# Tanh layer of a graph network: expansion in fp32 on 32 rows of the array, products as the stationary operand of the contraction, gathers not held back

## What is computed

```python
xs = concatenate([x[src, :8], x[dst, :8]])                 # 16 scalars of an edge
xv = concatenate([x[src, 8:], x[dst, 8:]])                 # 16 vectors of 3
h = 2.0 ** 0.5 * relu(emb @ W1 / 10.0 ** 0.5)              # 16 hidden values of an edge
w = (h @ W2 / 16.0 ** 0.5).reshape(E, 7, 16, 8)            # weights of an edge
s_out = PW_S * (einsum('eu,euw->ew', xs, wa_s) + INV_SQRT3 * einsum('eui,ei,euw->ew', xv, y1, wb_s))
g_out = PW_S * (einsum('eu,euw->ew', xs, wa_g) + INV_SQRT3 * einsum('eui,ei,euw->ew', xv, y1, wb_g))
v_out = PW_V * (...)                                       # 8 vectors of 3, from wc, wd and we
edge_ftr = concatenate([TANH_GAIN * tanh(s_out), TANH_GAIN * tanh(g_out)[:, :, None] * v_out]) * norm
out = segment_sum(edge_ftr, dst)
```

## Time and profile before

| | |
|---|---|
| median of 3 runs | 14886.34 us (14883.05 to 14889.52) |
| the profiled execution: its time, its span | 14891.23 us, 14889.4 us |
| the Tanh layer's pass, first to last expansion | 4499.3 to 9755.5 us |
| instructions in the span | 427370 |
| busy: PE, PEld, DVE, ACT, POOL | 79%, 61%, 87%, 53%, 67% |
| granted TensorE clock, mean of the span | 0.888 |

### The profile page before, as it was taken

One profiled execution on the slowest core, in us unless ns is written; L12 is line 12 of the kernel. 1 busy time (PEld: TensorE's weight loads), 2 busy tenths in 40 slices (PEclk: granted clock), 3 DMA queues, 4 the chain that ended last, 5 costly groups with the idle time before them and its releaser, 6 DMA issues. The chain is left out here.

```text
span 14889.4 us, 427370 instructions
## 1 busy us (share of the span) xinstructions
PE 11746.5 (79%) x109342; PEld 9054.7 (61%) x109342; DVE 12928.2 (87%) x30182; ACT 7888.3 (53%) x23572; POOL 9996.3 (67%) x10549
## 2 busy tenths in 40 slices
PE   1555555555548999999999999979788888888888
PEld 1444444444446666666666666667666666666666
DVE  5777777777768999999999999977799999999997
ACT  0555555555536666666666666638344444444443
POOL 4777777777756666666666666638577777777775
PEclk8666666666669999999999999979899999999999
DMA  3555555555542222222222222238211111111111
GB/s 94 84 87 87 86 87 86 87 87 87 87 67 38 36 36 36 36 36 36 36 36 36 36 36 36 36 116 293 57 24 24 24 24 24 24 24 24 24 24 23
DMA packets 2705891, 840.21 MB, mean 56 GB/s; under 512 B 2232498, under 2 KB 2650073, under 8 KB 2704124
## 3 DMA queue, kind: packets, MB, share of 16 engines
q1 hardware_dynamic: 2212179, 616.76, 20.7%
q0 software_dynamic: 312320, 178.52, 9.2%
q10 hardware_dynamic: 181250, 43.25, 1.3%
HBM read 610.22 MB, written 226.58 MB: 56 GB/s over the span
## 5 line engine op out<-in xcount | busy, mean ns | idle before, releaser
L1352 POOL DMA_INDIRECT w_rows<-table,w_idx x9375 | 8929.7, 952 | 4086.9 <-issue 2387.3
L1583 PE MATMUL w_p_w<-w_w,w_ht 128*128 128x256 f32 x12500 | 3007.2, 388 | 125.1 <-DVE w_prodv L1527 124.5
L1335 PE MATMUL w_p_deg<-w_hot_lo,w_hot_row 128*128 128x196 bf16 x6250 | 1797.5, 336 | 1573.4 <-DVE w_hot_lo L1280 1535.0
L1583 PEld LDWEIGHTS w_p_w<-w_w,w_ht 128*128 128x128 f32 x12500 | 2273.1, 190 | 673.5 <-issue 299.4
L1147 ACT ACTIVATE w_dist<-row_iota,w_negrel 128x32 f32<-128x32 f32 x9375 | 2182.6, 315 | 300.1 <-issue 272.2
L1554 ACT ACTIVATE w_ht<-w_p_h 128x512 f32<-128x512 f32 x1875 | 851.2, 526 | 2489.6 <-PE w_p_h L1574 2489.6
L1793 DVE TENSOR_TENSOR w_prod<-w_p_xe,w_he 128x512 f32<-128x512 f32 x3125 | 2137.5, 684 | 4.3 <-PE w_p_xe L1936 4.3
L1309 ACT CAST w_counts<-w_p_count 128x784 uint8<-128x784 f32 x1875 | 1247.2, 706 | 1453.3 <-PE w_p_count L1336 1435.9
L1335 PEld LDWEIGHTS w_p_deg<-w_hot_lo,w_hot_row 128*128 128x128 bf16 x6250 | 829.9, 133 | 1698.1 <-issue 1607.8
L1336 PE MATMUL w_p_count<-w_hot_lo,w_hot_row 128*128 128x196 bf16 x6250 | 1808.6, 336 | 0.0
L1959 PE MATMUL w_p_sgt<-w_prod,w_wc 128*32 128x128 f32 x25000 | 1331.6, 284 | 85.9 <-ACT w_sgt L1872 65.7
(11 more groups left out here) (211 smaller groups left out, 20273.9 us busy)
## 6 DMA issues: line engine op xcount, KB each, us to landing
counts<-w_counts SPq DMA_DIRECT2D x1250, 122.5 KB
d_small<-counts SPq DMA_DIRECT2D x388, 392.0 KB
w_rows<-table,w_idx POOLq DMA_INDIRECT x9375
w_rel_row<-rel_row SPq DMA_DIRECT2D x625, 120.0 KB
w_edge<-e SPq DMA_DIRECT2D x625, 80.0 KB
w_idx<-src SPq DMA_DIRECT2D x1875, 2.5 KB
w_negrel<-negrel SPq DMA_DIRECT2D x1875, 2.5 KB
w_nodes<-split SPq DMA_DIRECT2D x1875, 2.0 KB
```

Source lines behind the costliest of these rows:

```text
L1335: nc.tensor.matmul(p_deg[:], hot_row[s2][:, b, :], hot_lo[s2][:, b, :], start=False, stop=False, skip_group_check=True)
L1352: pool.indirect_dma_start(out=rows[:, t, :], out_offset=None, in_=table[0:N, :], in_offset=bass.IndirectOffsetOnAxis(ap=idx[:, t:t + 1], a ...
L1583: last = nc.tensor.matmul(p_w[(g.base * len(BANKS) + bank) % WBANKS][:, (t - t0) * 256:(t - t0 + 1) * 256], ht[g.slot(UNROLL)][:, k, t * P ...
```

## The change

Four things change in `window_pass_1`; the other layers keep their code.

1. The values are no longer split. PE turns `x32` itself, in fp32: five matmuls with `x32` (128 x 32) stationary and the fp32 identity moving, tile t into partitions 32 (t mod 4) of `p_xt`. ACT copies the result as fp32, in two instructions. Gone are ACT's two casts and DVE's two subtractions of a step.
2. `expand` multiplies in fp32: `pick_c` (32 x 128, on the partitions of the tile's strip) stationary, 128 columns of `xt` on the same 32 partitions moving; four matmuls a tile as before.
3. `contract` takes `prod` (128 x 128 fp32) as stationary operand and `wc` (24 columns) moving; four matmuls add up in `p_out[:, t, :]`, where the edges are on partitions at once. `p_sgt`, `sgt`, `stack`, ACT's two copies of a step and the five turning matmuls are gone; ACT takes tanh from `p_out` and copies its last 8 columns to `along`, from which DVE's L1826 now reads.
4. The five gathers of a group are issued without `wait_count` on the tile products.

```diff
@@ POOL
-                    for t in range(T):
-                        wait_count(pool, prod_ready, g.times(T, t - 3 * T))
-                        pool.nop(nofuse=True)
-                        gather_tile(pool, a["table"][1], idx[s], rows[s], t, gathered[s])
+                    pool.nop(nofuse=True)
+                    gather_rows(pool, a["table"][1], idx[s], rows[s], gathered[s])
@@ DVE
-                if g := at(2):
-                    vec.tensor_sub(rest[s2][:], x32[s2][:], xs[s2][:, :, 0, :]).then_inc(rest_ready, 1)
...
-                    vec.tensor_mul(prodv..., spread(p_out[:, :, T_AT:SGT], [P, T, 8, 3], 3),
+                    vec.tensor_mul(prodv..., spread(along[s2][:], [P, T, 8, 3], 3),
...
-                    vec.tensor_sub(xs[s2][:, :, 2, :], rest[s2][:], xs[s2][:, :, 1, :]).then_inc(low_ready, 1)
@@ ACT
                 if g := at(4):
-                    activate(g, 4, T)
+                    act.wait_ge(tile_out, g.times(T, T))
+                    nc.scalar.activation(bent[s2][:], p_out[:, :, 0:G_ROWS], ACT.Tanh, scale=1.0 / 32 ** 0.5).then_inc(bent_ready, 1)
+                    nc.scalar.copy(along[s2][:], p_out[:, :, T_AT:OUT]).then_inc(along_ready, 1)
...
-                    nc.scalar.copy(xt[g.slot(2)][0:SPLIT * 32, :], p_xt[:, 0:GE]).then_inc(xt_ready, 1)
-                if g := at(3):
-                    free(act, out_ready, g, 2)
-                    activate(g, 0, 4)
+                    nc.scalar.copy(xt[s2][:, 0, :], p_xt[:, 0, :])
+                    nc.scalar.copy(xt[s2][0:32, 1, :], p_xt[0:32, 1, :]).then_inc(xt_ready, 1)
@@ PE, expand
+                rows = slice(t % 4 * 32, t % 4 * 32 + 32)
                 for i in range(4):
-                    last = nc.tensor.matmul(p_xe[b][:, i * P:(i + 1) * P], pick_b[:, i, :], xt[g.slot(2)][:, t * P:(t + 1) * P],
+                    last = nc.tensor.matmul(p_xe[b][:, i * P:(i + 1) * P], pick_c[rows, i, :], xt[g.slot(2)][rows, t // 4, :],
                                             start=True, stop=True)
@@ PE, contract
                 for i in range(4):
-                    last = nc.tensor.matmul(p_sgt[QUAD * i:QUAD * (i + 1), t % 4 * P:(t % 4 + 1) * P], wc[:, i, :], prod[b][:, i, :],
-                                            start=True, stop=True)
-                last.then_inc(sgt_tile, 1)
+                    last = nc.tensor.matmul(p_out[:, t, :], prod[b][:, i, :], wc[:, i, :], start=i == 0, stop=i == 3)
+                last.then_inc(tile_out, 1)
@@ PE, step
-                if g := at(4):
-                    done(pe, sgt_last, g)
-                    for t in range(T):
-                        last = nc.tensor.matmul(p_out[:, t, :], sgt[g.slot(2)][:, t * P:(t + 1) * P], stack[:],
-                                                start=True, stop=True)
...
-                    for e in range(T):
-                        last = nc.tensor.matmul(p_xt[:, e * P:(e + 1) * P], xs[g.slot(2)][:, e, :, :].rearrange("p s i -> p (s i)"),
-                                                ident_b[:], start=True, stop=True)
+                    for t in range(T):
+                        last = nc.tensor.matmul(p_xt[t % 4 * 32:t % 4 * 32 + 32, t // 4, :], x32[g.slot(2)][:, t, :], a["ident"][:], start=True, stop=True)
```

More of the change, by code:

```diff
@@ L1658, in window_pass_1 @@
         dots = [sb(f"dots{s}", [P, T, MUL1, 3]) for s in range(2)]
-        xs = [sb(f"xs{s}", [P, T, SPLIT, 32], BF16) for s in range(2)]
-        rest = [sb(f"rest{s}", [P, T, 32]) for s in range(2)]
-        xt = [sb(f"xt{s}", [P, GE], BF16) for s in range(2)]
+        xt = [sb(f"xt{s}", [P, 2, P]) for s in range(2)]
         he = [sb(f"he{s}", [P, GE]) for s in range(UNROLL)]
@@ L1666, in window_pass_1 @@
         redv = sb("redv", [P, T, 24])
-        sgt = [sb(f"sgt{s}", [P, GE]) for s in range(2)]
         bent = [sb(f"bent{s}", [P, T, G_ROWS]) for s in range(2)]
-        stack = sb("stack", [P, WIDE])
+        along = [sb(f"along{s}", [P, T, 8]) for s in range(2)]
         gate = [sb(f"gate{s}", [P, T, 16]) for s in range(2)]
@@ L1723, in _ @@
         def _(pool):
-            pool.memset(pick_f[:], 0.0).then_inc(picks, 1)
+            pool.memset(pick_c[:], 0.0).then_inc(picks, 1)
             for b in range(4):
[L1727 to L1730, removed]
+                for q in range(4):
+                    pool.wait_ge(picks, 4 * b + q + 1)
+                    view = pick_c[:, b, :].rearrange("p (u h) -> p u h", h=HID1)
+                    pool.affine_select(out=view, in_=view, compare_op=ALU.not_equal, fill=1.0, base=-(32 * q + 8 * b),
                                        pattern=[[-1, 8], [0, HID1]], channel_multiplier=1).then_inc(picks, 1)
@@ L1791, in tile_products @@
                 dve.wait_ge(xe_ready, g.times(T, t + 1))
-                wait_count(dve, sgt_tile, g.times(T, t - 1))
+                wait_count(dve, tile_out, g.times(T, t - 1))
                 vec.tensor_mul(prod[b][:], p_xe[b][:].rearrange("p (i e) -> p i e", e=P),
@@ L1867, in _ @@
         def _(act):
[L1868 to L1872, removed]
             def step(at):
                 if g := at(4):
-                    activate(g, 4, T)
-                if g := at(2):
                     s2 = g.slot(2)
-                    done(act, q_ready, g)
-                    free(act, xt_mm, g, 2)
-                    nc.scalar.copy(xs[s2][:, :, 0, :], x32[s2][:]).then_inc(high_ready, 1)
+                    act.wait_ge(tile_out, g.times(T, T))
+                    free(act, gate_ready, g, 2)
+                    free(act, vout_ready, g, 2)
+                    nc.scalar.activation(bent[s2][:], p_out[:, :, 0:G_ROWS], ACT.Tanh, scale=1.0 / 32 ** 0.5).then_inc(bent_ready, 1)
+                    nc.scalar.copy(along[s2][:], p_out[:, :, T_AT:OUT]).then_inc(along_ready, 1)
                 if g := at(1):
@@ L1974, in step @@
                     expand(g, 1)
-                if g := at(4):
-                    done(pe, sgt_last, g)
-                    pe.wait_ge(dst_copied, g.times(1, 3) if at(2) else G)
-                    free(pe, w.acc_added, g, 1)
-                    for t in range(T):
-                        last = nc.tensor.matmul(p_out[:, t, :], sgt[g.slot(2)][:, t * P:(t + 1) * P], stack[:],
-                                                start=True, stop=True)
-                    last.then_inc(out_ready, 1)
-                if g := at(3):
-                    contract(g, 0)
-                    expand(g, 2)
-                    vector_weights(g, 0, 1)
                 if g := at(1):
@@ L1999, in step @@
                 if g := at(3):
+                    contract(g, 0)
+                    expand(g, 2)
+                    vector_weights(g, 0, 1)
                     contract(g, 1)
```

75 lines of the change are left out of this document (23 added, 52 removed).

## The result

The changed kernel takes 25106.54 us (median of 4 runs, 25097.27 to 25109.12); the kernel before, on the same chip, 14885.82 us (4 runs). The ratio is 1.687, 95% interval 1.684 to 1.689. Slower was forecast, but 18,280 us with a range of 17,500 to 20,500; the time lies near the rival with the lower clock (27,300 us).

What follows compares the result with a forecast made beforehand. PE was taken to bound the changed layer: 4.45 + 4.45 + 1.13 + 0.36 + 0.2 + 1.06 + 2.2 = 13.85 us a step against 8.42, over 625 steps 3394 us more: 18,280 us, range 17,500 to 20,500.

Steps and rivals of the forecast that it cites:

- the rival with the lower clock: Tanh layer: granted clock falls to 1.2 GHz, 28.3 us a step, 27,300 us if it lasts; chance 0.25.
- the sum: Tanh layer: PE's blocks and gaps at the upper clock, all on the path, add up to 13.85 us a step.
- the sums at 0.50: Sums after layers 0 and 1: granted clock 0.50 throughout, though PE is busy for 38.00 of 38 us.
- Fp32 loads: Expansion and contraction on PE: 0.111 us a load, paid twice per matmul, 4.45 us a step for each part.
- The gaps beside the expansion: PE between 32-row strips and the whole array: 11 gaps of 0.20 us, 2.2 us a step.
- DVE is covered: DVE in the Tanh layer: some 7.4 us of work a step, hidden by PE's 13.85; some 55% busy.
- The gathers cost nothing: POOL's gathers, no longer held for products: nothing gained, and running ahead costs nothing either.
- a faster kernel: Rival: a tile's four matmuls run side by side, PE needs 6.65 us, DVE sets the step, 14,250 us; chance 0.02.
- no change: Rival: only the freed gathers move the time, the rest is hidden, 14,890 us; chance 0.01.
- The rival without gaps: PE has no gaps between row strips and whole array: 11.65 us a step, 16,900 us; chance 0.06.
- The other layers keep their times: Sign: layers other than the Tanh layer should keep their times; otherwise something left out is at work.

Runs made afterwards that it cites:

- e4: Kernel before with only the fp32 expansion on 32 rows and the fp32 transposition; contraction, turn and held gathers as before: 23256.33 us.
- e11: Changed kernel with the contraction's moving operand padded with zeros to 96 columns, expansion still on 32 rows: 24608.21 us.
- e3: Kernel before with only the new contraction and the free gathers, bf16 expansion kept: 19253.06 us, ratio 1.293.
- e7: Kernel before with the new contraction and free gathers, wc padded with zeros from 24 to 96 columns: 14997.98 us, ratio 1.008.
- e2: Changed kernel with the expansion on all 128 rows, zeros outside the tile's strip: 17123.6 us.
- e1: Changed kernel with four bursts of 150 extra bf16 matmuls on 32, 64, 96 and 128 rows ahead of the Tanh layer: 25280.57 us.
- e5: Changed kernel with five extra bf16 matmuls of 128 rows and 512 columns ahead of each expansion, output overwritten: 21479.82 us.
- e8: Changed kernel with the gathers tied to the tile products again: 25100.81 us.
- e9: Kernel before with the Tanh layer's gathers issued at once, nothing else changed: 14877.52 us, ratio 0.9995.
- e10: Kernel before with the new contraction and free gathers, wc padded with zeros from 24 to 48 columns: 19331.38 us.

## Why the prediction was wrong

**The step that failed** is the assumption under the sum: that the granted clock stays at 1.00 in the layer, argued with "the expansion moves 128 columns, and half of the blocks are of that kind". It was 0.50. The argument took columns for what counts and the rows of the array for a side matter. The runs show that both matter, each by what runs beside it. With the expansion on 32 rows the layer is at 0.50 beside the old contraction (e4) and falls back to it beside one of 96 columns (e11). With the bf16 expansion it is at 0.50 beside 24 columns (e3) and at 1.00 beside 96 (e7). The 128 columns of the expansion do speak against the fall, but only on 128 rows (e2, where the 24-column contraction runs at 1.00 beside them). Gaps and fp32 alone are not the reason: the kernel before has gaps of 0.20 us at 1.00, and e2 multiplies in fp32 at 1.00. The level accounts for the miss: (24.8 - 13.85) x 625 = 6844 us, and the time lies 25,107 - 18,280 = 6827 us above the forecast. The warning stood in the text: the sums at 0.50, on 32, 64 and 96 rows with few columns and PE fully busy. They were read right as a rival and given 0.25; e1 would have told it from the forecast.

**The sum** holds at its own level, as far as the runs show it. Fp32 loads cost 0.111 us each twice over: 0.89 us a block on 128 rows in e2, and in e11 1.09 and 1.06 us for a block on 32 rows and one on the whole array, each with a gap. The gaps beside the expansion are real: 1.09 - 0.89 = 0.20 and 1.06 - 0.89 = 0.17 us. Two estimates for the whole step at 2.4 GHz lie near its 13.85 us: 13.5 from e5, and 12.03 + 5 x (2.15 - 2 x 0.89) = 13.9 from e2's step and e11's blocks. No run holds the change at 1.00 without other work added, so that it would take the forecast's 18,280 us there is argued and not shown. The page "TensorEngine Tiling (Array Packing)" of the Trainium skill says in Key Properties that a change of mode drains the engine. The blocks that are longer by 0.20 and 0.17 us agree with that; no row records a drain as such.

**The clock rival** named what happened and overpriced it: 28.3 us a step against 24.8. Its 0.231 us a load came from `f_part`; the change's loads measured 0.208, 80 x 0.023 = 1.8 us of the 3.5. Its gaps of 0.38 were too long as well: an expansion and a contraction with their gaps took 9009.32 - 9005.49 = 3.83 us, where the rival has 16 x 0.231 + 2 x 0.38 = 4.46. Over five tiles loads and gaps together make some 3.1 us of the 3.5.

**The rest.** DVE is covered, as forecast: it waits for PE (6514.7 us), and is 32% busy in place of some 55% because the step is longer. The gathers cost nothing at either end (e8, e9). The rivals of a faster kernel and of no change are out by the time. The rival without gaps is out by the blocks of e11, which have gaps at 1.00. The other layers keep their times: from the last expansion to the end of the span it is 14889.4 - 9755.5 = 5133.9 us before and 25106.1 - 19982.0 = 5124.1 us with the change.

No run with the new expansion or contraction beats the kernel before. e7 comes nearest and is 0.8% slower: its step is 2000 x 40/9296 = 8.61 us, with PE and DVE both busy 95% or more.

## What to carry to other kernels

Before costing a matmul stream by its pitch, look at the granted clock of the stretches in the same trace that resemble it in rows, in moved columns and in loads per matmul: a change that fills the array less can nearly double the price of a load (0.111 to 0.208 us here), and the vector weights and the message sum, which it does not touch, run at the lower level too. If a stage sits at 0.50 with PE fully busy, zeros on all 128 rows or as more moving columns are worth a run: e2 and e7 gained 7983 and 4255 us by them, while 48 columns (e10) gained nothing and 96 columns beside 32 rows (e11) little. In e2 the zeros cost no load time: the pitch stayed at 0.111 us.

## What was not expected of the hardware

- Busy is not enough: bf16 matmuls of 512 columns back to back took 626 and 631 ns on 32 and 64 rows at 0.50, and 403 and 379 ns on 96 and 128 rows (the first of the 96 still at 0.50).
- More work was faster: 7983 us by zero rows (e2), 4255 by zero columns (e7 against e3), 3627 by matmuls whose result is thrown away (e5).
- The level is no property of one instruction. The 24-column contraction ran at 1.00 beside the 128-row fp32 expansion (e2) and at 0.50 beside the bf16 one (e3). What the chip adds up is open: the runs show 32, 64, 96 and 128 rows in bursts, and 24, 48 and 96 columns in this layer, and nothing between.
